# One attention-and-feed-forward layer on one core: the written-out order of jobs between the score products is replaced, heads trail by two units over four probability buffers, and the step loop is written out

## The reference, cut to what matters

```python
h = token_table[x] + segm_table[mask] + pos             # 8 x 1024 x 192, float32
# attention on layernorm(h): 12 heads of 16, each row attends to its own batch row of 1024 positions
qkv = layernorm(h) @ qkv_weight.T
q, k = layer_norm(q) * 16 ** -0.5, layer_norm(k)        # per head, over 16 values
h = h + (softmax(q @ k.T) @ v) @ proj_weight.T
# feed-forward on layernorm(h), with rounded and clipped values of 4 bits
xq = round(clip(layernorm(h) / a1, -8, 7)); wq1 = round(clip(w1 / alpha_w1, -8, 7))
x1 = clip(gelu(xq @ wq1.T * alpha_w1 * a1 + b1), -10, 10)   # 768 hidden
hq = round(clip(x1 / a2, -8, 7));            wq2 = round(clip(w2 / alpha_w2, -8, 7))
h = h + hq @ wq2.T * alpha_w2 * a2 + b2
```

## Time and profile before

| what | value |
|---|---|
| device time, median of 3 runs (lowest to highest) | 1224.66 us (1220.38 to 1228.03) |
| the profiled execution | 1228.44 us |
| its span, first to last instruction | 1226.6 us |
| mean granted TensorE clock | 0.959 of full |
| PE busy | 1016.1 us (83%) |
| ACT busy | 864.9 us (71%) |
| DVE busy | 818.1 us (67%) |
| POOL busy | 436.9 us (36%) |

### The profile page before, as it was taken

The page is one execution under the profiler, slowest core; times in us unless marked ns, Lnnn a source line. Parts: engine busy times, 40 slices in busy tenths (PEclk is TensorE's granted clock), DMA queues, the critical chain, the costliest instruction groups (busy, mean ns, idle before and its releaser), DMA issues.

```text
span 1226.6 us, 21889 instructions
## 1 busy us (share of the span) xinstructions
PE 1016.1 (83%) x7535; PEld 370.1 (30%) x7535; DVE 818.1 (67%) x2289; ACT 864.9 (71%) x936; POOL 436.9 (36%) x354
## 2 busy tenths in 40 slices
PE   1247898989988898898999898898889898989883
PEld 1133233333333333232333332233333333322231
DVE  6385747768686767668686777658676776834355
ACT  0146687778787778668777778668777777788861
POOL 3655241433535343342535243243534321301011
PEclk9977999999999999899999999899999999999995
DMA  7712020010202010020202011020202000000000
GB/s 195 169 15 27 1 27 1 20 21 1 40 1 39 2 30 11 17 26 1 40 1 35 6 27 14 3 40 1 40 1 30 11 14 1 2 14 1 14 13 13
DMA packets 26711, 29.66 MB, mean 24 GB/s; under 512 B 5057, under 2 KB 23169, under 8 KB 26593
## 3 DMA queue, kind: packets, MB, share of 16 engines
q0 software_dynamic: 18432, 12.59, 8.8%
q1 hardware_dynamic: 7184, 14.86, 3.6%
q10 hardware_dynamic: 976, 0.70, 0.3%
HBM read 21.85 MB, written 6.29 MB: 23 GB/s over the span
## 4 chain that ended last, share of the span: by engine, by line
PE 41%; DVE 27%; ACT 16%; issue 12%; POOL 2%; DMA 2%; DVEq 0%; ACTq 0%; POOLq 0%; SPq 0%
PE ps_o L904 14%; ACT probs L533 13%; PE ps_s L887 7%; PE ps_j L932 4%; DVE gelu L681 4%; PE ps_j L984 3%; PE ps_j L940 3%; DVE gelu L680 3%; PE ps_j L970 3%; DVE sq L651 2%; PE ps_j L951 2%; DVE qT L698 2%; DVE stack L659 2%; DVE kT L698 2%; PE ps_j L955 2%
## 5 line engine op out<-in xcount | busy, mean ns | idle before, releaser
L533 ACT ACTIVATE probs<-ps_s 128x1024 f32<-128x1024 f32 x768 | 733.2, 1024 | 180.1 <-PE ps_s L887 178.9
L904 PE MATMUL ps_o<-probs,v_sb 128*32 128x512 f32 x3072 | 421.6, 616 | 1.4 <-ACT probs L533 0.5
L887 PE MATMUL ps_s<-qT,kT 64*128 64x512 f16 x1536 | 272.8, 392 | 65.8 <-ACT probs L533 50.0
L456 POOL TENSOR_TENSOR stack<-sq,stack 128x384 f16<-128x384 f32 x128 | 131.3, 1046 | 159.8 <-DVE stack L659 159.8
L887 PEld LDWEIGHTS ps_s<-qT,kT 64*128 64x128 f16 x1536 | 61.9, 94 | 322.8 <-ACT probs L533 281.6
L465 POOL TENSOR_TENSOR gelu<-gelu,b_row 128x768 f32<-128x768 f32 x16 | 29.1, 1816 | 310.5 <-DVE gelu L733 310.5
L527 ACT ACTIVATE gelu<-ps_j,b_sb,s_sb 128x512 f32<-128x512 f32 x96 | 69.7, 774 | 80.4 <-PE ps_j L970 80.1
L403 POOL DMA_INDIRECT h_all<-in_L_tok_token_table,idx x64 | 99.8, 1560 | 71.2 <-DMA h_all<-in_L_tok_segm_table,idx 56.6
L403 POOL DMA_INDIRECT h_all<-in_L_tok_segm_table,idx x64 | 99.8, 1560 | 26.1 <-issue 15.1
L666 DVE COPY o_sb<-ps_o 128x512 f32<-128x512 f32 x48 | 33.1, 689 | 91.6 <-PE ps_o L904 91.6
L447 POOL TENSOR_TENSOR sq<-parts 128x384 f32<-128x384 f32 x28 | 23.2, 827 | 193.0 <-DVE parts L696 193.0
(11 more groups left out here) (125 smaller groups left out, 1098.1 us busy)
## 6 DMA issues: line engine op xcount, KB each, us to landing
h_all<-in_positions SPq DMA_DIRECT2D x8, 768.0 KB, 6.1
out<-h_all SPq DMA_DIRECT2D x16, 384.0 KB, 2.3
qT<-in_L_ffn_w SPq DMA_DIRECT2D x2, 576.0 KB, 8.9
h_all<-in_L_tok_segm_table,idx POOLq DMA_INDIRECT x64, 4.6
h_all<-in_L_tok_token_table,idx POOLq DMA_INDIRECT x64
probs<-in_L_attn_qkv_weight SPq DMA_DIRECT2D x2, 432.0 KB, 4.5
probs<-in_L_ffn_alpha_a ACTq DMA_DIRECT2D x1, 384.0 KB, 5.5
probs<-in_L_attn_proj_weight SPq DMA_DIRECT2D x1, 144.0 KB, 5.3
```

Source lines behind the costliest of these rows:

```text
L456: last = nc.gpsimd.tensor_tensor(low, src, high, ALU.subtract)
L533: nc.scalar.activation(probs[:, u % 2, 2 * pair:2 * pair + 2], ps_s[:, 2 * pair:2 * pair + 2], ACT.Exp, scale=SCORE_SCALE).then_inc(exp_do ...
L887: last = mm(ps_s[:, j], kT[rows, par, head // 2, m * P:(m + 1) * P], qT[rows, par, head // 2, nh * NQ:(nh + 1) * NQ], start=True, stop=True)
L904: last = mm(ps_o[32 * j:32 * j + 2 * D, :], v_sb[:, par, m, (GH * group + j) * VE:(GH * group + j) * VE + 2 * D], probs[:, u % 2, j], star ...
```

## The change

- `PLAN` is another table. `heads` is now a word of it (`h`), so that it can stand anywhere in a unit, twice or not at all; the `t`-th `h` of a step is `heads(t - 2)`, and the first two are the last two units of the step before. `o` is a word too, and `g` marks the unit before whose exponentials ACT runs the gelus (it is 13 still).
- `probs` has four buffers instead of two.
- `o_nat` (with `xf`), `hn`, `y_sb`, `qk`, `xq` and `xqT` have memory of their own. The waits that guarded the shared memory go: gelu and the first norm no longer wait for `out_ready`, and n of tile 0 no longer waits for the last X.
- `h_all` is a ring of 8 halves. The start loads `positions` 4 times instead of 8; SP loads the other four later, each behind two stores of the result, after a wait for them.
- All 18 steps are written out on every engine, with constants in the waits.

```diff
-G3 H0 ; H1
-H2 ; H3 l0
+h h o
+Y0 Y1 Y2 F0 Y3 w0 F1
...
+PROBS = 4
+HEADS_BEHIND = 2
...
-        h_all = sb("h_all", [P, B * TB * C])
-        probs = sb("probs", [P, 2, GH, NQ])
+        h_all = sb("h_all", [P, RING * TH * C])
+        probs = sb("probs", [P, PROBS, GH, NQ])
...
+        o_nat, hn, y_sb = (sb(n, [P, TH, C]) for n in ("o_nat", "hn", "y_sb"))
+        xf = o_nat
+        qk = sb("qk", [P, TH, 2 * C])
...
+        xq = sb("xq", [P, TH, C], BF16)
+        xqT = sb("xqT", [KC, 2, NQ], BF16)
...
-            for s in range(2):
-                one(s, s, s // 2)
-            with eng.Fori(0, (B - 2) // 2) as turn:
-                for k in range(4):
-                    one(2 + k, turn * 4 + (2 + k), turn * 2 + (1 + k // 2))
-            for s in range(HALVES - 2, HALVES + 2):
+            for s in range(HALVES + 2):
                 one(s, s, s // 2)
...
-            for b in range(1, B):
+            for b in range(1, RING // 2):
                 load_pos(b)
...
+                if y % 2 and (y + RING) // 2 < B:
+
+                    sp.wait_ge(stored, 16 * (y + 1))
+                    load_pos((y + RING) // 2)
...
-                if j == 0 and job_runs("Y", s0):
-
-                    act.wait_ge(out_ready, nth(job_half("Y", s), 0, 1))
...
-                if t == 0 and job_runs("X", s0):
-
-                    dve.wait_ge(job_mm["X"], nth(job_half("X", s), HB - 1, HB))
...
+                    for kind, t in UNIT_WORK[u]:
                         if kind in job_mm:
                             job(s0, s, kind, t)
+                        elif kind == "h" and t >= HEADS_BEHIND and attends(s0):
+                            heads(s0, s, t - HEADS_BEHIND)
+                        elif kind == "h" and t < HEADS_BEHIND and attends(s0 - 1):
+
+                            heads(s0 - 1, s - 1, UNITS + t - HEADS_BEHIND)
```

More of the change, by code:

```diff
@@ L38 @@
 HALVES = 2 * B
+RING = 8
 KC = C // 2
@@ L75 @@
 PLAN = """
[L76 to L80, removed]
-G3 H0 ; H1
-H2 ; H3 l0
[L83 to L98, removed]
+h h o
+Y0 Y1 Y2 F0 Y3 w0 F1
+G0 F2 F3 H0 G1 P0
+h h
+G2 G3 W0 W1 W2 H1 H2 H3
+h l0 h R0
+W3 m0 h
+W4 h
+h N0 W5 I0
+I1 h o A0
+I2 h A1 A2
+h A3 I3
+C0 B0 X0
+X1 B1 r0 X2 X3 B2 X4 X5 r1 B3 h r2 h r3 g h
+h
+h S0 n0
+h n1 o
+D0 x0 E0 C1
+n2 h C2 D1
+E1 n3 h
+D2 h x1
+h D3 E2 x2
+E3 x3 x4 h
+x5 C3 h
 """
 JOB_KINDS = "ABCDEFGHIWXY"
[L103 to L107, removed]
+UNIT_WORK = [[] for _ in range(UNITS)]
+TAKEN = {"h": 0, "o": 0, "g": 0}
+for unit_work, unit_line in zip(UNIT_WORK, PLAN.strip("\n").split("\n")):
+    for word in unit_line.split():
+        if word in TAKEN:
+            unit_work.append((word, TAKEN[word]))
+            TAKEN[word] += 1
+        else:
+            unit_work.append((word[0], int(word[1])))
+JOBS = [w for unit in UNIT_WORK for w in unit if w[0] in JOB_KINDS]
+GELU_UNIT = next(u for u, unit in enumerate(UNIT_WORK) if ("g", 0) in unit)
+PROBS = 4
+HEADS_BEHIND = 2
 FIRST_PLAN = """
@@ L403, in gather @@
                     nc.gpsimd.indirect_dma_start(
-                        out=h_all[:, t * C:(t + 1) * C], out_offset=None, in_=table,
+                        out=h_tile(half, j), out_offset=None, in_=table,
                         in_offset=bass.IndirectOffsetOnAxis(ap=idx[:, which, t:t + 1], axis=0),
@@ L483, in _ @@
                 split_low(s, s)
-            for s in range(HALVES + 2):
-                one(s, s, s // 2)
+            halfsteps(one)
         @block.scalar
@@ L548, in _ @@
                     square(s, s, t)
-            halfsteps(act, one)
+            halfsteps(one)
         @block.vector
         def _(dve):
-            steps = {"done": 0, "turns": 0}
+            steps = {"done": 0}
             def link(ins):
@@ L559, in link @@
                 ins.then_inc(dve_step, 1)
-                dve.wait_ge(dve_step, steps["turns"] + steps["done"])
+                dve.wait_ge(dve_step, steps["done"])
             ts = nc.vector.tensor_scalar
@@ L841, in _ @@
                 work(s, s, kind, t)
-            for s in range(2):
-                one(s, s)
-            before = steps["done"]
-            with dve.Fori(0, (B - 2) // 2) as turn:
-                steps["turns"] = turn * LINKS_PER_TURN
-                for k in range(4):
-                    one(2 + k, turn * 4 + (2 + k))
-            assert steps["done"] - before == LINKS_PER_TURN, steps["done"] - before
-            steps["turns"] = ((B - 2) // 2 - 1) * LINKS_PER_TURN
-            for s in range(HALVES - 2, HALVES + 2):
+            for s in range(HALVES + 2):
                 one(s, s)
```

75 lines of the change are left out of this document (28 added, 47 removed).

## The result

The changed kernel takes **1112.47 us** (median of 4 runs, 1112.17 to 1113.33) against 1225.77 us (4 runs of the kernel before on that chip). The ratio is 0.908, 95% interval 0.906 to 0.911.

A forecast was written before the change was run, and what follows sets the result against it. No engine is full; waits between engines in order set the step. Steady steps 53, step 0 1.5, steps 14 and 15 2, loop 9.9, clock 4: 70.4 off 1224.7 gives 1154 us, range 1118 to 1192.

The forecast's parts named there:

- Y to H: Front of a steady step, units 1 to 4 after unit 1's scores: 12.8 us, all PE, DVE hidden behind it.
- up to here nothing is won: First Y to the end of unit 12's exponentials: 30.2 us against 29.7 before, with the same PE work.
- 58.9 in both tables: PE's summed work per step, claimed to be 58.9 us in the old table and the new.
- Rival 1: Steady steps: waits vanish further, down to the unit sum of 61.4 a step, 34 less, 1120 us; chance 0.13.
- H3 to t: From the last H to the end of unit 12's exponentials (t): 17.4 us.
- C's departure: C jobs leave unit 13; in step 0, which has no X, this alone was to gain 1.5 us.
- Rival 2: DVE's tail runs longer than its sum through meetings with POOL: 2.5 a step, +33, 1187 us; chance 0.22.
- The loop: Two turns of the hardware loop, costing 9.9 us together, go when the steps are written out.
- Rival 4: Slower: PE idles 2.5 before Y0, then 2.3 of slow products, 15 steps, 72 us, 1226 and up; chance 0.05.
- The clock: Six steps at 69.5 instead of 68.1 carry 8 us; half, 4, was taken as gain.
- Four buffers and own buffers: nothing: Four probs buffers and separate memory remove only waits for things long past: 0 us.
- The ends: Start, 0 of up to 2 us; step 0, 1.5; steps 14 and 15, 1 each; closing tail, 0.

The follow-up runs named there:

- experiment 4: Changed kernel with jobs in their new units, but heads one unit behind and one in every unit: 1220.55 us, ratio 0.997 to the kernel before.
- experiment 3: Changed kernel (own buffers, ring, four probability buffers, steps written out) with the old table and heads one behind put back: 1210.57 us, ratio 0.988 to the kernel before.
- experiment 7: Changed kernel with its jobs and heads two behind, but one heads in every unit: 1183.39 us, ratio 0.969 to the kernel before.
- experiment 2: Kernel before, loop kept, with all jobs of units 1 to 6 ahead of that unit's heads: 1216.69 us, ratio 0.994.
- experiment 10: Changed kernel with H1 moved between G2 and G3 in unit 4: 1115.76 us, ratio 0.912 to the kernel before.
- experiment 5: Changed kernel with C0 to C3 put back in unit 13, behind B3: 1124.85 us, ratio 0.921 to the kernel before.
- experiment 9: Changed kernel with C2 moved from unit 18 to unit 23, behind x5: 1120.55 us, ratio 0.916 to the kernel before.
- Experiment 1: Kernel before with only its 18 steps written out; table, buffers and waits stay: 1211.71 us, ratio 0.989.
- experiment 11: Changed kernel run again unaltered on the same chip as the follow-up runs: 1113.55 us, ratio 0.910 to the kernel before.
- experiment 8: Changed kernel with the new table's units 0 to 11 and the old jobs from 12 on, one heads in each of these, two behind: 1154.96 us, ratio 0.946.

## Why the prediction was right in direction and wrong in size

The steps at full clock, as front + back, in the order in which the parts come in (experiment 4 has no step at full clock; 1.6 of its front is the lower one). The jobs' new places alone are worth 0.8 at full clock (68.8 less 1.6 is 67.2), the lag then 1.4 more, the `heads` in free places 4.4:

| kernel | heads | front | back | step |
|---|---|---|---|---|
| experiment 3, old table | one behind, one a unit | 29.1 | 38.9 | 68.0 |
| experiment 4, new places of jobs | one behind, one a unit | 33.8 | 35.0 | 68.8 |
| experiment 7 | two behind, one a unit | 30.3 | 35.5 | 65.8 |
| changed kernel | two behind, free places | 27.4 | 34.0 | 61.4 |

- **The step that failed is "Y to H", and with it "up to here nothing is won".** I priced 12.8 for it, and 30.2 from Y's start to t, where the table before took 29.7. Measured: 10.8 and 28.1. The costs of Y, F, G and H from the earlier trace rows were the dearest of each, read where a job stands beside `heads` or `scores`, and I carried them into a table in which jobs stand in rows. By the starts in PE's timeline these 16 jobs take 8.5 in a clean step before and 7.4 in the changed kernel; I had priced them 9.1 in both. The 24 `heads`, priced 24.0, take 24.0 and 23.3 (1.00 alone, 0.93 in pairs, 0.91 in the three of unit 13). Three experiments move the costs the same way: jobs grouped in the old table (experiment 2, 0.8 less busy time), `heads` taken apart in the new one (experiment 7, 1.1 more), and a single H moved (experiment 10, 0.2 more).
- **PE's work "58.9 in both tables" was wrong for the new one.** Summed by starts, with the waits left out, its products come to about 56.5, and to about 58.4 before. The busy time that the rows show is 2.5 above that in both (59.0 and 60.9). So the 1.9 by which 58.9 fell short of the busy time of 60.8 was no sign of this error, and that the new busy time came out at 59.0 does not confirm the old sum.
- **Rival 1 (0.13) named the step of 61.4, and that is luck.** Its 61.4 was the sum of units, each the larger of ACT and PE, at my prices. With the measured 10.8 for 12.8 the same rule gives 59.4, and the step is 2.0 longer. The waits on top of the sum, 2.6 in the forecast, did not vanish as that rival has it; the products were cheaper. Its counter-argument held: DVE's tail is there, at t + 33.2, and Y comes right behind it.
- **H3 to t** (17.4; measured 17.2), **exponentials 13** (from t + 7.4; t + 7.5), **the tail** (t + 33.5; t + 33.2) and **t to Y** (33.8; 33.3) were right to 0.5. **C's departure** was right in direction; its return costs 0.8 a step (experiment 5). The wait at D2 was set at 1.3 and is 0.16. Most of its cover is C2: without it, it is 1.04 (experiment 9).
- **Rival 2** (longer DVE tail) did not come, though the meetings moved. Behind S, before, six DVE instructions are long beside POOL (four of them x), together 3.3 over their usual time. In the changed kernel there are six again (three x, three of n), together 3.2.
- **The loop**: 9.9 forecast. Experiment 1 gives 12.3 of time for it: the turns, a step less at 0.98, and 0.2 in each step, where I took nothing for the register instructions (no run shows that they are the cause). Right in size, but the earlier trace rows were misread. Its `heads` of 1.92 is half a `heads` (4 of 8 records). The other half stands behind it, and the whole takes 3.9:

```profile
507.49 1.92 PE L904 MATMUL ps_o<-probs,v_sb 128*32 128x512 f32 x4 [0.16 <-issue]
```

  At the lower clock a whole `heads` takes 1.9 (experiment 4). So more than the clock slows it at a turn, and what, stays open. Rival 4 took its 2.3 of slow products from here; behind the wait for o in experiment 4 they cost 1.6.
- **The clock** was put at 8 and halved (4). The six steps at 69.5 that it counts are five in the trace, 7.4 in all, and all of that came back. I kept half for a new wait that is not there.
- **"Four buffers and own buffers: nothing"** holds for their memory alone (experiment 3). It leaves out what the lag that they allow is for: from experiment 4 to 7 the front loses 3.5, of which 1.6 is the lower clock behind the wait for o. I had `heads(8)` waiting 0.4 for o in my sum, so the term was in it rightly, but nothing in my text says that one behind would make it 2.7.
- **The ends** were undersized. Start to the first steady step: 232.3 to 219.6, 12.7, of which I had 5.6 (1.5 for step 0, 4.1 for step 1). The first exponential comes 3.6 earlier, of which the ring with its four transfers fewer has 0.8 to 2.0 (97.5 to 98.5 in all kernels that have it, 99.25 and 99.55 in experiments 1 and 2), and I took 0 of "up to 2"; the rest is the one profile before, which no experiment repeats. Steps 14 and 15: 121.7 to 115.0 (116.3 in experiment 11), 6.7 for my 2; their front is 26.6 for 28.8 in experiment 3.

The sum of the misses: twelve steps by 2.5 each, 30 (2.0 of the 2.5 is Y to H); clock 3 to 4; the start with steps 0 and 1, 7; steps 14 and 15, 5; what is behind them, 1; together 46. Forecast were 70.4, measured are 116.4 in span.

What stays open: why a product costs less behind its own kind; and what makes the lower clock skip a step. In experiments 3 and 7 a wait of 1.6 to 1.7 stands in every step, and slow products stand behind it in four and in five of the twelve. Two kernels were not run: the old table with heads two behind, and experiment 4 with o ahead of N on DVE. So it is not shown that the lag pays without the new places, nor that the wait for o needs the lag to go.

## What to carry to other kernels

A cost read from a trace belongs to its place in the queue. Before you price a reordered table, read each job's cost from start to start at several places, with other neighbours, and take the range (F was 0.33 to 0.48) and not one row. Sum starts and not busy times: here the busy time lay 2.5 above the sum in both tables. Price both the unit sum and each chain of dependencies. Then ask of every wait in the sum what fills it: a job ahead of a wait is nearly free (C2), and moving it to a bound unit costs its full length. Where a result is emptied by another engine between two products (o between `heads(7)` and `heads(8)`), test placements and lag apart: here the placements alone came out slower than the old table, since they opened a wait of 2.6 and the lower clock with it.

## What the hardware showed that was not expected

- The same fp32 products on PE cost by their neighbours: `heads` 0.93 in pairs and 1.00 alone, be it between jobs or between `scores`; H 0.69 in a row, 0.75 with a job on one side, 0.85 between `heads` and `scores`; F 0.33 between two Y, 0.48 between `heads` and `scores`.
- Every slow product looked up in steady steps stands within 4 us behind an idle time of 1.6 to 3.0 on PE (1.62, 1.68, 2.46, 2.66 and 3.04), with a `heads` at 1.9 for 1.0 when no turn is near: the lower level, 1.2 GHz. Not every such idle time is followed by one: in experiment 8 PE waits 1.5 to 1.6 for `o_sb` in each step, and all its steady steps are at 1.00, like those of the changed kernel, where no wait is over 0.6. In step 14 of the changed kernel a slow `heads` stands 3 us behind a wait of only 1.17 for a gelu.
- Straight code for 18 steps shows no wait for instructions on PE in the steady steps: the list of its waits above holds three other engines only. The Trainium skill, "Runtime: NRT & Kernel Launch", section Instruction fetch mechanics, says that sequential code is fetched ahead and mostly hidden; this trace agrees.
